# Order of ScalarE's work and the row of d, in a graph layer with a normalised 4096 x 4096 adjacency

## The reference

```python
rowsum = adj.sum(axis=1)
d_inv_sqrt = jnp.where(rowsum > 0, rowsum ** (-0.5), 0.0)
normalized_adj = d_inv_sqrt[:, None] * adj * d_inv_sqrt[None, :]
h = jnp.maximum(_layernorm(x, axis=-1), 0.0)
out = x + relu(normalized_adj @ h @ W + b)
```

## Time and profile before

| | us |
|---|---|
| median of 3 runs | 411.45 |
| lowest, highest | 410.63, 412.59 |
| the profiled execution's own time | 411.19 |
| its span, first to last instruction | 409.4 |

### The profile page before, as it was taken

How to read it: one execution, slowest core, us unless ns; L and a number is a source line. 1 busy time by engine, 2 the same in 40 slices (tenths; PEclk the granted TensorE clock), 3 DMA queues, 4 the chain that set the end, 5 groups by cost and what they waited for, 6 DMA issues and landing times.

```text
span 409.4 us, 5217 instructions
## 1 busy us (share of the span) xinstructions
PE 395.6 (97%) x1792; PEld 328.4 (80%) x1792; DVE 313.6 (77%) x316; ACT 288.8 (71%) x283; POOL 116.5 (28%) x273
## 2 busy tenths in 40 slices
PE   7897999999998999999999999999999999999995
PEld 6785887878887888888888888888888888888884
DVE  4667848788795886958598796958588494899996
ACT  2779678787889767877679787767777756335532
POOL 2272435262323601542335115522333130000000
PEclk9999999999999999999999999999999999999999
DMA  8999999999999999999999999996999455387663
GB/s 280 426 416 423 420 418 422 421 420 422 423 420 422 420 419 420 419 415 359 404 399 380 384 383 426 418 395 255 391 418 407 208 205 208 153 349 268 204 207 154
DMA packets 22617, 147.40 MB, mean 360 GB/s; under 512 B 2624, under 2 KB 2880, under 8 KB 6208
## 3 DMA queue, kind: packets, MB, share of 16 engines
q1 hardware_dynamic: 22592, 147.07, 89.6%
HBM read 142.87 MB, written 4.19 MB: 359 GB/s over the span
## 4 chain that ended last, share of the span: by engine, by line
PE 73%; DMA 14%; ACT 4%; issue 3%; DVE 2%; POOL 2%; SPq 1%; POOLq 0%; DVEq 0%
PE moved L725 17%; PE moved L727 17%; PE moved L726 17%; DMA nat<-in_adj 11%; PE held L727 6%; PE held L725 6%; PE held L726 6%; PE moved L694 3%; DMA at<-in_x 3%; ACT hi L374 2%; DVE lo L570 1%; ACT nat L361 1%; PE moved L743 1%; PE moved L678 1%; ACT G L386 0%
## 5 line engine op out<-in xcount | busy, mean ns | idle before, releaser
L570 DVE SCALAR_TENSOR_TENSOR lo<-at,s,hi 128x1024 fp32r<-128x1024 f32 x112 | 141.3, 1278 | 25.1 <-ACT hi L374 25.0
L725 PE MATMUL moved<-hi,G 128*128 128x512 f32 x384 | 150.9, 393 | 4.7 <-DVE acc L586 2.2
L374 ACT ACTIVATE hi<-at,s 128x1024 fp32r<-128x1024 f32 x112 | 122.7, 1142 | 40.7 <-issue 38.8
L727 PE MATMUL moved<-hi,G 128*128 128x512 f32 x384 | 150.1, 391 | 0.0
L726 PE MATMUL moved<-lo,G 128*128 128x512 f32 x384 | 149.9, 390 | 0.0
L589 DVE TENSOR_TENSOR acc<-moved,acc 128x1024 f32<-128x1024 f32 x84 | 102.7, 1222 | 52.2 <-PE moved L727 52.0
L361 ACT ACTIVATE nat<-nat 128x2048 f32<-128x2048 f32 x64 | 122.2, 1910 | 24.8 <-DMA nat<-in_adj 24.8
L725 PEld LDWEIGHTS moved<-hi,G 128*128 128x128 f32 x384 | 72.5, 189 | 21.7 <-DVE acc L586 3.0
L727 PEld LDWEIGHTS moved<-hi,G 128*128 128x128 f32 x384 | 72.4, 189 | 15.2
L726 PEld LDWEIGHTS moved<-lo,G 128*128 128x128 f32 x384 | 72.5, 189 | 15.0
L489 POOL TENSOR_TENSOR row_sum<-part 128x1 f32<-128x1 f32 x32 | 16.0, 499 | 162.2 <-ACT nat L361 162.2
(11 more groups left out here) (55 smaller groups left out, 238.2 us busy)
## 6 DMA issues: line engine op xcount, KB each, us to landing
nat<-in_adj SPq DMA_DIRECT2D x64, 1024.0 KB, 11.9
at<-in_adj_t SPq DMA_DIRECT2D x64, 1024.0 KB, 8.3
turned<-in_x SPq DMA_DIRECT2D x4, 512.0 KB, 12.2
nat<-in_x_t SPq DMA_DIRECT2D x4, 512.0 KB, 4.7
turned<-in_x_t SPq DMA_DIRECT2D x4, 512.0 KB, 5.4
out<-nat SPq DMA_DIRECT2D x4, 512.0 KB, 4.1
at<-in_x SPq DMA_DIRECT2D x3, 512.0 KB, 9.1
out<-turned SPq DMA_DIRECT2D x3, 512.0 KB, 4.4
```

Of the source, the lines that this page charges most:

```text
L374: nc.scalar.activation(hi[g % RING][:, 2 * c:2 * c + 2, :], at[g % LA][:, 2 * c:2 * c + 2, :], ACT.Copy, scale=s[:, j:j + 1]).then_inc(hi_ ...
L570: nc.vector.scalar_tensor_tensor(out=lo[g % RING][:, tiles, :], in0=at[g % LA][:, tiles, :], scalar=s[:, j:j + 1], in1=hi[g % RING][:, til ...
L725: nc.tensor.matmul(into[:, f, :], big, hi[g % RING][:, t, :], start=begins, stop=False)
L727: mm = nc.tensor.matmul(into[:, f, :], small, hi[g % RING][:, t, :], start=False, stop=ends)
```

## The change

It has three parts. (1) In ScalarE's iteration g the cast of slot g+2 comes ahead of the iteration's sums, except where slot g+2 is the first of its step; chunk 1's cast in iteration 1 comes after both. (2) The table of sums adds its extra half in iterations 24, 31, 38, 45 and 52, and none before 24. (3) `turn_d` and `take_d_rows` go. SP stores d to DRAM after the load of slot 58, when all scales are made, waits for the store, and loads it twice as half a row of 2048 onto all 128 partitions, in nat buffers 0 and 1. For this the rows are dealt out as (p j) in place of (j p): tile j holds rows 32p + j, p being the partition. Neighbouring partitions of a natural half then read from rows 32 apart (512 KB), not adjacent ones (16 KB). `adj_t` and x are laid out for it on the host.

```diff
-        end = min(2 * WIDTHS[0] + min(2 * (g + 1), g + 3) + g // 8, 2 * NB)
+        end = min(2 * WIDTHS[0] + min(2 * (g + 1), g + 3) + max(0, g - 17) // 7, 2 * NB)
...
-    adj_rows = adj.rearrange("(j p) (c k) -> j c p k", p=P, k=HALF)
+    adj_rows = adj.rearrange("(p j) (c k) -> j c p k", p=P, k=HALF)
...
-        def d_row(pos):
-            r = pos // 2
-            start = (r % 2) * 2 * PW + (pos % 2) * PW
-            return nat[r // 2][:, start:start + PW]
...
+        def d_row(i):
+            n = HALF // PW
+            return nat[i // n][:, i % n * PW:(i % n + 1) * PW]
...
+            def save_d():
+                sp.wait_ge(s_ready, NB)
+                sp.dma_start(d_dram, d[:, :]).then_inc(d_saved, DMA)
+
+            def spread_d():
+
+                sp.wait_ge(d_saved, DMA)
+                row = d_dram.rearrange("p j -> (p j)").rearrange("(o r) -> o r", o=1)
+                for e in range(2):
+                    half = row[:, e * HALF:(e + 1) * HALF]
+                    sp.dma_start(nat[e][:, :], half.to_broadcast([P, HALF])).then_inc(d_row_landed[e], DMA)
...
+                if g == BASE[LAST]:
+                    spread_d()
                 if q == 0 and k in LOADING:
                     load_x(LOADING[k])
...
                 if g + 3 < len(SLOTS):
                     load_slot(g + 3)
+                if g == BASE[LAST] - 1:
+                    save_d()
...
-            def take_d_rows(r):
-                act.wait_ge(d_turned, r + 1)
-                act.wait_ge(nat_summed, 2 * NB)
-                nc.scalar.copy(d_rows(r), pair_of(("d_row", r))[:, :, :]).then_inc(d_row_ready, 1)
...
             for g, (k, q, _) in enumerate(SLOTS):
-                if g == 1:
-                    round_raw(1)
+
+
+                ahead = g + 2 < len(SLOTS) and SLOTS[g + 2][1] != 0
+                if ahead:
                     round_slot(g + 2)
                 for m in NATS[g]:
                     sum_nat(m)
-                if g != 1 and g + 2 < len(SLOTS):
+                if not ahead and g + 2 < len(SLOTS):
                     round_slot(g + 2)
+                if g == 1:
+                    round_raw(1)
...
-                if k == LAST - 1 and q == 0:
-                    for r in range(NP // 2):
-                        take_d_rows(r)
...
             def scale_rows(pos):
                 i = panel_order(LAST)[pos]
-                dve.wait_ge(d_row_ready, pos // 2 + 1)
+                dve.wait_ge(d_row_landed[i * PW // HALF], DMA)
...
-                if k == LAST - 1:
-                    turn_d(2 * pos)
-                    turn_d(2 * pos + 1)
```

More of the change, by code:

```diff
@@ L121, in at_least, with build @@
         eng.wait_ge(sem, value)
-def build(nc, x, x_t, adj, adj_t, w, b, out):
+def build(nc, x, x_t, adj, adj_t, w, b, d_dram, out):
     N, D = adj.shape[0], w.shape[0]
@@ L192, in h @@
             return flat.rearrange("p (t f) -> p t f", f=D)
-        def d_row(pos):
-            r = pos // 2
-            start = (r % 2) * 2 * PW + (pos % 2) * PW
-            return nat[r // 2][:, start:start + PW]
-        def d_rows(r):
-            return nat[r // 2][:, (r % 2) * 2 * PW:(r % 2 + 1) * 2 * PW].rearrange("p (a k) -> p a k", k=PW)
+        def d_row(i):
+            n = HALF // PW
+            return nat[i // n][:, i % n * PW:(i % n + 1) * PW]
         def x_out(pos):
@@ L218, in build @@
         at_landed = [sem(f"at_landed{e}") for e in range(LA)]
+        d_saved = sem("d_saved")
+        d_row_landed = [sem(f"d_row_landed{e}") for e in range(2)]
         x_out_landed = [sem(f"x_out_landed{e}") for e in range(LX)]
@@ L242, in build @@
         taken = sem("taken")
-        d_turned = sem("d_turned")
-        d_row_ready = sem("d_row_ready")
         scaled = sem("scaled")
@@ L280, in build @@
                     use(("project", c), gathered % ROT, signal, count)
-                if pos < HELD and k == LAST - 1:
-                    for q in range(2 * pos, 2 * pos + 2):
-                        use(("d_row", q), (gathered + q) % ROT, d_row_ready, q + 1)
         def pair_of(key):
@@ L603, in scale_rows @@
                     whole = held[i][:, f, :] if i < HELD else total(pos)[:, f, :]
-                    nc.vector.tensor_tensor(out=total(pos)[:, f, :], in0=whole, in1=d_row(pos),
+                    nc.vector.tensor_tensor(out=total(pos)[:, f, :], in0=whole, in1=d_row(i),
                                             op=ALU.mult).then_inc(scaled, 1)
@@ L733, in multiply @@
                     mm.then_inc(panel_done, 1)
[L735 to L745, removed]
             def amid(k, pos):
@@ L781 @@
     n, dim = x.shape
-    blocks = adj.reshape(NP, PW, NB, P)
-    slots = [blocks[panels, :, FIRST[k]:FIRST[k] + WIDTHS[k], :].transpose(3, 2, 0, 1).reshape(P, SLOT, PW)
+    blocks = adj.reshape(NP, PW, P, NB)
+    slots = [blocks[panels, :, :, FIRST[k]:FIRST[k] + WIDTHS[k]].transpose(2, 3, 0, 1).reshape(P, SLOT, PW)
              for k, _, panels in SLOTS]
     arrays = {
-        "in_x": np.ascontiguousarray(x.reshape(NP, BW, P, dim).transpose(0, 2, 1, 3)),
+        "in_x": np.ascontiguousarray(x.reshape(P, NP, BW, dim).transpose(1, 0, 2, 3)),
         "in_x_t": np.ascontiguousarray(x.reshape(NP, PW, dim // P, P).transpose(0, 3, 2, 1)),
@@ L795 @@
             for name, a in arrays.items()]
+    d_dram = nc.dram_tensor("d_dram", (P, NB), F32).ap()
     out = nc.dram_tensor("out", arrays["in_x_t"].shape, F32, kind="ExternalOutput").ap()
-    build(nc, *args, out)
+    build(nc, *args, d_dram, out)
     r = run_bass_kernel_spmd(nc, [arrays], core_ids=[0])
```

## The result

The changed kernel takes 406.22 us (median of 6 runs, 405.38 to 407.76) against 411.11 us (6 runs, 410.63 to 412.59): ratio 0.988, 95% interval 0.9852 to 0.9909. Its runs fall in two groups of three: 405.38, 405.42, 405.43 with a mean granted clock of 0.999 to 1.000, and 407.00, 407.05, 407.76 with 0.995. The profiled execution is one of the lower group: 405.38 us, span 403.6, 5.8 us under that of before.

What follows compares the result with a forecast made beforehand. TensorE, busy 395.6 of 409.4 us, was taken to bound the kernel, with DMA full past 110 us. Terms 0.5 + 2.3 + 3.5 - 0.9 - 0.2 = 5.2 off 411.19 gave 406.0 us, range 403.5 to 409.5.

Steps and rivals of the forecast that it cites:

- The start: Iteration 0: slot 2's cast starts 0.83 us earlier; TensorE restarts at 37.5 after 1.4 us idle instead of 2.2.
- the gate: Step 1's last panel: TensorE waits from 71.0 to 73.1 us on natural half 12; lead shrinks to 0.5 us.
- After the gate: The second gather wait (0.8 us) and the wait for ScalarE's turned copy (1.45) both go: +2.3 us.
- Slot 24: Iteration 24's two sums hold up the turned copy; a new TensorE wait, 0.7 + 0.2: cost 0.9 us.
- The row of d: Two blocks of sixteen transposes leave TensorE, +3.5 us; store and loads have 9 us of cover, cost 0.
- The last tile's G: Made one iteration later, its two operations now ahead of a last-step gather: cost 0.2 us.
- The sum: 0.5 + 2.3 + 3.5 - 0.9 - 0.2 = 5.2 us off the profiled 411.19, giving 406.0 us.
- Rival 1: The clock falls at the gate; eight matmuls at 0.43 us add 1.6, giving 407.6 us; chance 0.20.
- list (a): TensorE stops at 35.76, 2.17 us idle, then eight matmuls at 1.2 GHz, some 1.6 us more.
- The pitch: 512 KB between partitions slows natural loads: 407.1 by the skill's ratio, about 429 us at x = 0.3; chance 0.21.
- the late row: Row of d lands over 9 us late, VectorE passes the delay on: slower than 411 us; chance 0.04.

Runs made afterwards that it cites:

- the order alone: Kernel before with only ScalarE's new order of casts and sums: 410.77 us (12 runs) against 411.01, ratio 1.000.
- the table alone: Kernel before with only the new table of sums: 408.84 us (6 runs) against 411.01, ratio 0.9938.
- the gate filled: Changed kernel with nine zero-tile matmuls ahead of TensorE's wait in step 1's last panel: 405.26 us (5 runs).
- the gate open: Changed kernel with slot 8's cast ahead of natural half 12's sum in iteration 6 too: 404.38 us (4 runs), ratio 0.9836.
- 16 KB pitch: Changed kernel with natural halves read at the old 16 KB between partitions: 407.49 us (5 runs).
- late row: Changed kernel with the wait and two loads of d's row moved behind slot 60's load: 411.59 us (10 runs), ratio 1.001.
- order undone: Changed kernel with ScalarE's old order, new table and row of d by DRAM kept: 405.55 us (4 runs), ratio 0.9859.
- turned copy first: Changed kernel with ScalarE's copy of a turned chunk ahead of the iteration's sums: 404.49 us (5 runs), ratio 0.9853.
- row alone: Kernel before with only the row of d by way of DRAM, no transposes of d: 407.61 us (6 runs) against 411.01, ratio 0.9907.

## Why the prediction was right, point by point

- **The start.** The restart came at 36.63 after 0.97 us, not at 37.5 after 1.4: slot 2 landed a little sooner (its cast starts at 32.97, for 33.84). A second wait of 0.42 us, at 40.08, was not in the forecast. As forecast, the lead ends at the gate; with the order alone no change of the time could be told.
- **The gate.** Idle 2.07 us for 2.1 forecast. That the two agree so closely is in part luck: TensorE came there 0.8 us sooner than forecast (70.2 for 71.0) and was released 0.7 us sooner (72.44 for 73.1), and in the other profiles with this gate the wait was between 1.73 and 2.56 us. Opening it took its wait and about 1 us away, less than 1.8; the profiled execution lost some 1 us of that in slot 12, 1.36 us of waiting where 0.4 was worked out from landings that I took as fixed. The fastest run, 403.93, is near the 403.6 forecast.
- **After the gate.** The two waits went, +2.3 forecast, and the table alone measured 2.2.
- **Slot 24.** Idle 0.67 us, and 1.06 - 0.23 + 0.1 = 0.9 lost, as forecast. Moving the copy gave it back.
- **The row of d.** +3.5 forecast, 3.4 measured alone. The store took 3.9 us, not 2.5, but the last scale was ready at 341.4 and not at 345 (the last sum ended at 339.3 for 341.9 forecast, and POOL's six operations took 2.0 us, not 3.1: in the earlier trace rows one of them had taken about 1 us longer), so the cover was 9.7 us, not 9. The last tile's G cost 0.15 + 0.1 us for 0.2.
- **The sum.** 5.2 forecast and 5.8 between the profiled executions. The rest is put down to the landing of half 12, 66.88 against 67.55 us: it varies from run to run by more than that (66.5 to 68.0), and behind the gate everything moves with it.
- **The clock, mis-sized.** Rival 1 said 407.6 at a chance of 0.20. It came in 6 of 12 runs, at 407.0 to 407.8, so its chance was too low. That its mechanism was right is argued from three things: the runs with the gate filled or open have no upper group, the two groups differ in the mean clock as they should, and two kernels with the same gate (16 KB pitch, late row) show the fall there in their profiles. Both profiles of the changed kernel itself are of the lower group. Nor is the length of the idle time all that decides: these two fell behind 2.56 and 2.48 us, but waits of 2.28, 2.32 and 2.51 us elsewhere passed without a fall. The median of 406.2 lies between two groups, neither of which is there. That it matches the forecast of 406.0 owes something to this.
- **Falls that cost nothing.** I had priced the fall at 39 us in the kernel before at 1.6 us in list (a). It is made good at the next waits: of nine runs of the kernel before on one chip, the five at a mean clock of 0.993 or 0.994 took 410.66 to 411.77 us, the four at 0.996 to 0.999 took 411.16 to 411.50.
- **The pitch and the late row.** The first didn't come: 4.97 us for a half and a slot at either pitch, and the 207 to 214 GB/s that the Trainium skill (page "DMA: Bandwidth & Descriptors", section "Latency and other measured facts") gives for HBM copies does not carry over to these loads, which go into SBUF in pieces of 8 KB; by that ratio they would have come 4.89 apart at 16 KB. The late row is real at its price, 4.4 us of 4.8, but stayed 9.7 us away.

## What to carry to other kernels

Before crediting an earlier start, look for the next point that is set by a full DMA queue: a lead ends there, and so do the losses ahead of it. Where an engine both feeds the path and does bookkeeping for later, let the feeding go first everywhere, and check the one iteration in which doubled bookkeeping meets another task. A median that lies between two groups of runs says less than the groups; here nine idle-filling matmuls pointed to what splits them.

## What the runs showed of the hardware

- TensorE's clock fell to its 1.2 GHz level (steps of 0.43 us for 0.23) behind waits of 2.17 (before), 2.19 (order undone), 2.48 (late row) and 2.56 us (16 KB pitch), and did not behind 2.07 (changed kernel), 2.18 (table alone), 2.28 (order alone), 2.32 (turned copy first) and 2.51 us (row alone). Behind the waits of 1.74 us and less in the steps no timeline shows a fall. Among the longer ones the length alone does not tell which will; what else counts is open. Matmuls with a zero tile in a wait's place kept the clock up.
- Up to 110 us, with the DMA engines full, all loads landed in the order of their issue in all thirteen profiles, mostly 2.48 us behind the one before for a megabyte. Single landings came up to 1.6 us later than that, and what was behind them was late too; this, and where the train of loads stands at 20 us, is why half 12's sum starts anywhere from 66.5 to 68.0 us. From 20 us on, each such jump of 0.6 us or more stands within 5 us behind a packet of the queues that the page lists as instruction, mostly one of 16 KB that took about 1.05 us, with an 8 KB packet of a load right behind it that took 0.8 where most take 0.31. For half 14 with the gate open the packet started at 74.0 us. Other such packets passed without a jump, as at 80.3 us in the changed kernel, so that they are the cause is not shown.
- A 16 KB store of 128 rows of 128 bytes took 2.6 to 4.8 us to land in the ten profiles that have it. With the row loaded ahead of slot 59, 1 MB read from one 8 KB row onto 128 partitions took 4.6 us in the changed kernel, and the second one landed 2.45 us behind the first, the pace of any other megabyte.
